# An attention layer and a routed feed-forward network on one core: constant rows of the stacks written by the engines, and three orders in the passes changed

## The reference

```
qkv = x @ W_attn + b_attn                      # 256 -> 768
scores = where(causal & (j >= i - 64), q.k / 4, -inf)
x = layernorm(x + softmax(scores) @ v @ W_proj + b_proj)
e = argmax(softmax(x @ Wr.T))                  # one expert a row
inter = gelu(x @ W1[e] + b1[e])                # 256 -> 1024
y = layernorm(inter @ Wo + bo + x) * gamma + beta
out = layernorm(x + y)
```

## Time and profile before

| | us |
|---|---|
| median of 3 runs (lowest, highest) | 550.52 (549.26, 554.35) |
| the profiled execution, its own time | 547.5 |
| its span in the profile | 545.5 |
| PE busy, share of the span | 494.5, 91% |
| DVE, ACT, POOL busy | 421.4, 353.8, 320.6 |

### The profile page before, as it was taken

How to read it: one execution, slowest core, us unless ns; L and a number is a source line. 1 busy time by engine, 2 the same in 40 slices (tenths; PEclk the granted TensorE clock), 3 DMA queues, 4 the chain that set the end, 5 groups by cost and what they waited for, 6 DMA issues and landing times. The chain is left out here.

```text
span 545.5 us, 24637 instructions
## 1 busy us (share of the span) xinstructions
PE 494.5 (91%) x8593; PEld 435.1 (80%) x8593; DVE 421.4 (77%) x1117; ACT 353.8 (65%) x800; POOL 320.6 (59%) x570
## 2 busy tenths in 40 slices
PE   4579999999999999989897899898999999999890
PEld 3458888888888888878786689897999999999780
DVE  3437888898788885886886647899999999888583
ACT  3437777768686785674756487665667667677560
POOL 7801444445453464443526456788888888888584
PEclk9959999999999997997988999999999999999896
DMA  9697676787786968687567112222343266244510
GB/s 209 166 240 190 169 205 183 225 236 183 205 217 184 248 188 219 178 227 175 145 163 194 37 42 80 61 81 71 93 100 96 81 218 228 81 146 156 179 27 14
DMA packets 97353, 83.72 MB, mean 153 GB/s; under 512 B 37447, under 2 KB 88784, under 8 KB 97235
## 3 DMA queue, kind: packets, MB, share of 16 engines
q1 hardware_dynamic: 93874, 73.70, 49.7%
q0 software_dynamic: 3264, 8.41, 4.5%
q10 hardware_dynamic: 96, 0.04, 0.0%
HBM read 43.63 MB, written 23.62 MB: 123 GB/s over the span
## 5 line engine op out<-in xcount | busy, mean ns | idle before, releaser
L1683 PE MATMUL ps<-wo_hi,ks 128*128 128x256 f16 x576 | 129.5, 274 | 4.3 <-DVE ks L1269 4.0
L1701 PE MATMUL ps<-sT_hi,w_hi 128*128 128x128 f16 x496 | 104.9, 220 | 0.4 <-issue 0.4
L1701 PE MATMUL ps<-sT_lo,w_hi 128*128 128x128 f16 x496 | 105.0, 220 | 0.0
L1701 PE MATMUL ps<-sT_hi,w_lo 128*128 128x128 f16 x496 | 105.0, 220 | 0.0
L1146 DVE TENSOR_REDUCE mx<-ps 128x4 bf16<-128x512 f32 x128 | 82.7, 683 | 8.8 <-PE ps L1469 8.2
L666 POOL CAST att_hi<-att 128x256 f16<-128x256 f32 x32 | 12.7, 396 | 123.9 <-DVE att L974 123.9
L1683 PE MATMUL ps<-wo_lo,ks 128*128 128x256 f16 x288 | 78.8, 274 | 0.0
L816 ACT ACTIVATE probs<-ps 128x512 f32<-128x512 f32 x128 | 69.4, 612 | 6.6 <-PE ps L1495 5.9
L1372 PE MATMUL ps<-v_even,probs 128*64 128x17 f32 x1024 | 71.5, 212 | 1.4 <-issue 1.4
L1372 PE MATMUL ps<-v_odd,probs 128*64 128x17 f32 x1024 | 71.5, 212 | 0.3 <-issue 0.3
L1372 PEld LDWEIGHTS ps<-v_even,probs 128*64 128x64 f32 x1024 | 66.8, 141 | 5.1 <-issue 4.5
(11 more groups left out here) (266 smaller groups left out, 1531.4 us busy)
## 6 DMA issues: line engine op xcount, KB each, us to landing
qk_s<-qk_hi SPq DMA_DIRECT2D x64, 128.0 KB, 3.0
w_in<-in_L_ffn_W_dram SPq DMA_DIRECT2D x32, 256.0 KB, 4.0
v_odd<-slots SPq DMA_DIRECT2D x62, 128.0 KB, 2.1
qs<-qk_s SPq DMA_DIRECT2D x16, 384.0 KB, 4.3
ks<-qk_s SPq DMA_DIRECT2D x16, 384.0 KB, 5.2
ks<-qk_s SPq DMA_DIRECT2D x32, 144.0 KB, 3.9
v_even<-v_odd SPq DMA_DIRECT2D x63, 68.0 KB, 4.2
qk_s<-qk_lo SPq DMA_DIRECT2D x32, 128.0 KB, 3.5
```

Source lines behind the costliest of these rows:

```text
L1683: ins = mm(ps_y[p], h[p][hs][:, ic, :], wo[ws][:, ic, :], start=n == 0, stop=n == 3 * IC - 1)
L1701: up_ins = mm(ps_h[1 - p][:, half, col + m * width:col + (m + 1) * width], weights(ws, owners[m], k, ic), sT[1 - p][ss][:, k, at], start=k ...
```

## The change

- The identity and the mask are built by POOL in the layout of the stacks, 128 rows high, `ident_w` first. DVE derives `odd` (one per row: whether it is a constant row) and copies `ident_w` over the whole of `qs[0]` and `qs[1]`. `key_rows` takes the place of `last_rows` at full height, and the `window_rows` copies now write all 128 rows of `ks`. `constant_rows` and its six DMAs are gone.
- The copies must be done before the stacks' even rows are loaded: `stacks_begin` waits for them. ACT's copies are spread over passes -4 and -3, DVE's too; POOL has one block of four copies in place of two.
- `w1` is loaded and split one pass later: half `it + 2` is loaded in pass `it`, half `it` split in it; the last split (pass 31) stands early on DVE.
- The early table is spread over passes 26, 27 and 28, in 26 and 27 behind `qk_lo`.
- In passes 28 to 31 (`ending`) the value product stands behind the transposes of the maxima, and `turn_attention` behind `scores_t(1)`.

The core of the diff:

```diff
-            sp.wait_ge(zeros_done, 1)
-            sp.wait_ge(masks_done, 1)
-            constant_rows(0)
...
                 wait(sp, st_done, 4 * (2 * g - 2))
+                if g < 2:
+                    sp.wait_ge(query_rows_done, g + 1)
+                    sp.wait_ge(window_done[g], 2)
...
-                for n in (0, 1) if it == -2 else (it + 3,) if a_tile(it + 3) and it > -2 else ():
+                n = it + 2
+                if a_tile(n):
...
-                if it == FIRST + 2:
-                    constant_rows(1)
...
+            low, high = slice(0, ALIGNED), slice(ALIGNED, P)
+            link(nc.gpsimd.memset(ident_w, 0.0))
+            link(nc.gpsimd.affine_select(out=of_copies(low, BLK), ...
+            nc.gpsimd.affine_select(out=of_copies(high, BLK), ... .then_inc(ident_w_done, 1)
...
+            for rows, per, first, last in ((low, 2, 1, P - 1), (high, 1, -STACK, P - BLK // 4)):
+                for sign, base in ((1, first), (-1, last)):
+                    link(nc.gpsimd.affine_select(out=mask_w[rows, :], ...
+            link(nc.gpsimd.affine_select(out=mask_w[high, :], ...
+            pool.wait_ge(odd_done, 1)
+            link(nc.gpsimd.tensor_scalar(mask_w[low, :], mask_w[low, :], odd[low, :], 1.0 / ONE, ALU.mult, ALU.mult))
+            for b in range(2):
+                link(nc.gpsimd.tensor_copy(key_rows[:, b, :, :, :], ...
+                nc.gpsimd.affine_select(out=key_rows[high, b, :, :, :], ... .then_inc(last_done, 1)
...
-                n = it + 1
+                n = it
                 if a_tile(n):
                     piece, cols = n // 2, slice(n % 2 * I // 2, (n % 2 + 1) * I // 2)
                     act.wait_ge(w1_ld[n % 2], 16 * (n // 2 + 1))
...
-                if it == FIRST + 1:
-                    act.wait_ge(last_done, 1)
-                    for e, t in ((0, 0), (0, 1), (1, 0), (1, 1)):
-                        last = nc.scalar.activation(window_rows(0, 0, e, t), last_rows[:, 0, :, :, :], ACT.Copy)
+                if it in (FIRST, FIRST + 1):
+                    act.wait_ge(last_done, 2)
+                    for t in range(2):
+                        last = nc.scalar.activation(window_rows(0, 1, it - FIRST, t), key_rows[:, 1, :, :, :], ACT.Copy)
...
-            nc.vector.memset(ks[0][0:ALIGNED, 0, :, 0:BLK], 0.0).then_inc(zeros_done, 1)
+            dve.wait_ge(ident_w_done, 1)
+            nc.vector.tensor_reduce(odd[:, :], ident_w[:, 0:BLK], AX.X, ALU.max).then_inc(odd_done, 1)
+            for k in range(2):
+                nc.vector.tensor_copy(qs[k][:, :, :], ident_w.unsqueeze(1).broadcast_to([P, HEADS, 2 * P]))\
+                    .then_inc(query_rows_done, 1)
...
-                if it == EARLY_OF + 2:
-                    early_runs()
-                    early_entries()
...
+                if it < EARLY_OF + 4:
+                    early_table(it)
...
+                ending = it >= TILES - LEAD
...
+                if a_tile(it + 1) and not ending:
+                    v_product(it + 1)
...
                 queries_keys(range(2 * CC))
                 if it == LAST:
                     first_up(first_owner, range(IC // 4, IC // 2))
+                elif ending:
+                    v_product(it + 1)
...
-                if it == LAST:
+                if ending:
                     turn_attention(done, ps_attT)
```

More of the change, by code:

```diff
@@ L286, in attention_then_routed_ffn @@
         xin_ld = [sem(f"xin_ld{k}") for k in range(3)]
-        rows_st = [sem(f"rows_st{k}") for k in range(2)]
+        query_rows_done = sem("query_rows_done")
         qk_st = [sem(f"qk_st{k}") for k in range(2)]
@@ L588, in _, with of_copies @@
                                     base=0, pattern=[[-1, P]], channel_multiplier=1).then_inc(ident_done, 1)
+            low, high = slice(0, ALIGNED), slice(ALIGNED, P)
+            def of_copies(rows, n):
+                return ident_w[rows, :].rearrange("p (t k) -> p t k", k=n)
+            link(nc.gpsimd.memset(ident_w, 0.0))
+            link(nc.gpsimd.affine_select(out=of_copies(low, BLK), in_=of_copies(low, BLK), compare_op=ALU.not_equal, fill=ONE,
+                                         base=-1, pattern=[[0, 4], [-2, BLK]], channel_multiplier=1))
+            nc.gpsimd.affine_select(out=of_copies(high, BLK), in_=of_copies(high, BLK), compare_op=ALU.not_equal, fill=ONE,
+                                    base=STACK, pattern=[[0, 4], [-1, BLK]], channel_multiplier=1).then_inc(ident_w_done, 1)
+            pool.wait_ge(ident_w_done, 1)
             nc.gpsimd.memset(bqk[:, :], 0.0).then_inc(bqk_clear, 1)
@@ L591, in _ @@
             link(nc.gpsimd.memset(mask_w, 0.0))
[L593 to L602, removed]
+            for rows, per, first, last in ((low, 2, 1, P - 1), (high, 1, -STACK, P - BLK // 4)):
+                for sign, base in ((1, first), (-1, last)):
+                    link(nc.gpsimd.affine_select(
+                        out=mask_w[rows, :], in_=mask_w[rows, :], compare_op=ALU.is_ge, fill=MASKED, base=base,
+                        pattern=[[sign * per, P]], channel_multiplier=-sign))
+            link(nc.gpsimd.affine_select(out=mask_w[high, :], in_=mask_w[high, :], compare_op=ALU.is_ge,
+                                         fill=0.0, base=MROWS - ALIGNED - 1, pattern=[[0, P]], channel_multiplier=-1))
+            pool.wait_ge(odd_done, 1)
+            link(nc.gpsimd.tensor_scalar(mask_w[low, :], mask_w[low, :], odd[low, :], 1.0 / ONE, ALU.mult, ALU.mult))
+            for b in range(2):
+                link(nc.gpsimd.tensor_copy(
+                    key_rows[:, b, :, :, :], mask_w.unsqueeze(1).unsqueeze(1).broadcast_to([P, STRIPS, CC, P])))
+                nc.gpsimd.affine_select(
+                    out=key_rows[high, b, :, :, :], in_=key_rows[high, b, :, :, :], compare_op=ALU.not_equal, fill=-ONE,
+                    base=ALIGNED - MROWS - STRIPS * b, pattern=[[-1, STRIPS], [-2 * STRIPS, CC], [0, P]],
+                    channel_multiplier=1).then_inc(last_done, 1)
+                pool.wait_ge(last_done, b + 1)
             link(nc.gpsimd.tensor_copy(ident_b[:, :], ident[:, :]))
@@ L1156, in router_x, with low_weights @@
                     nc.vector.tensor_tensor(lx[:, m % 4, :], ps_v[:, C:C + E], lb[:, :], ALU.add).then_inc(lx_done, 1)
+                def low_weights(n):
+                    piece, cols = n // 2, slice(n % 2 * I // 2, (n % 2 + 1) * I // 2)
+                    dve.wait_ge(w1h_done, n + 1)
+                    nc.vector.scalar_tensor_tensor(w1s[1][:, piece, cols], w1_in[:, cols], W_UP,
+                                                   w1s[0][:, piece, cols], ALU.mult, ALU.subtract)\
+                        .then_inc(w1l_done, 1)
                 maxima(0)
                 maxima(1)
+                if it == LAST:
+                    low_weights(it)
                 for t in turned(it):
@@ L1182, in _ @@
                     nc.vector.tensor_scalar(wr_in[:, :], wr_in[:, :], wr_mean[:, :], None, ALU.subtract).then_inc(centre_step, 1)
+                    dve.wait_ge(last_done, 1)
+                    for e, t in ((0, 0), (0, 1), (1, 0), (1, 1)):
+                        last = nc.vector.tensor_copy(window_rows(0, 0, e, t), key_rows[:, 0, :, :, :])
+                    last.then_inc(window_done[0], 1)
                 if it == 1:
```

109 lines of the change are left out of this document (43 added, 66 removed).

## The result

The changed kernel takes 557.15 us (median of five runs, 555.22 to 559.84); the kernel before, timed beside it, 549.26 (548.55 to 554.35). The ratio on record is 1.0246, 95% interval 1.0192 to 1.0300: slower, though whether by 2% or more stays unclear. Here that is 1.0144 with no execution left out on either side, and what makes 1.0246 of it can't be worked out from the times; that the kernel is slower doesn't hang on it, for the lowest of its five executions (555.22) lies above the highest of the kernel before (554.35). The profiled execution took 557.1 us (span 555.3) against 547.5 (545.5), 9.6 more.

What follows compares the result with a forecast made beforehand. TensorE sets the pace, so only its idle stretches and clock count. Start -4.2, early table -3.0 and end +3.4 sum to -3.8 us, taking 550.5 to 546.7; range 539.5 to 553.5.

Steps and rivals of the forecast that it cites:

- End of the passes: Passes 28 to 30: new order and late slot rows lose 3.4 us, bounds 0.5 gained and 5 lost.
- Maxima rows later by 0.7: Passes 28 to 30: `v_odd` waits for the later value product ahead of the maxima rows on ScalarE, 0.7 us late.
- 0.3 more: Passes 28 to 30: `scores_t(3)` shares a bank with `attT`, waits for turn and VectorE's copy, 0.3 us.
- For three passes 2.1: Passes 28 to 30: the new order's delays of 0.4 to 1.0 us each, 2.1 us lost together.
- Slot rows 1.3: First slot rows, queued behind the last `w1` load in pass 29, make TensorE wait 1.3 us.
- Constant rows: Start: engines replace six DMAs; stack load issued at 21.5 to 24.5 us, first scores at 27.2.
- Weights: Start: later weight units remove the 3.84 us hole; x tile 4 waits 0.5; transposes 2.3 us earlier; other passes cost nothing.
- The clock at the start: Half of 7.8 us behind the start's hole gets 2.4 GHz: 1.95 us gained, bounds none or 3.9.
- Early table: Around pass 26: spreading the table removes a wait for `qk_lo`, 3.0 us gained, bounds 0 and 3.3.
- Rival 2: Start: full-height blocks hold each other up on VectorE and GpSimd, scores near 33 us; 554.7 us, chance 0.13.
- Rival 1: Better than forecast: the end costs nothing and the clock stays high; 10.5 us faster, 540.0 us, chance 0.27.
- Rival 3: Middle passes: late stack loads in the queue give back the start's 4.2 us; 550.9 us, chance 0.18.

Runs made afterwards that it cites:

- e1: The changed kernel with TensorE's old order restored in passes 28 to 31; 547.84 us, ratio 1.0009 to the kernel before.
- after: The changed kernel itself, with all parts of the change, against the kernel before; 557.15 us, ratio 1.0246.
- e3: The changed kernel with ScalarE's `v_odd` copy behind the maxima rows in passes 28 to 31; 553.96 us, ratio 1.0081 to the kernel before.
- e7: The changed kernel with 24 unread products in each of TensorE's waits for maxima rows and slot rows; 557.04 us, ratio 1.0158 to the kernel before.
- e10: e3 plus `early_table(28)` ahead of `router_x` on VectorE and first slot rows read before the last `w1` load; 551.45 us, ratio 1.0038.
- e5: e1 plus first slot rows read ahead of the last `w1` load in pass 29; 547.68 us, ratio 0.9941 to the kernel before.
- e8: e5 plus 36, 44, 22 and 22 idle products in four TensorE waits of the start; 546.36 us, ratio 0.9946 to the kernel before.
- e9: The kernel before with only the early table spread over passes 26 to 28; 549.43 us, ratio 0.9996.
- e12: e5 plus 30, 30, 14, 14 idle products at the start and 18 before `turn_attention` in passes 28 to 30; 547.50 us, ratio 0.9938.
- e2: The kernel before with only the new order of passes 28 to 31; 557.49 us over four runs, no ratio.
- e6: The kernel before with only the weight units loaded and split one pass later; 551.76 us, ratio 1.0051.
- e4: The kernel before with only the constant rows made by the engines; 551.36 us, ratio 0.9987.

## Why the prediction was wrong

Forecast were 546.7 us and most likely no change; it is 557.15, 3.6 us above the range's upper end. Step by step:

**End of the passes: the step that failed.** The waits are the ones forecast: the value product behind the transposes, `v_odd` ahead of the maxima rows on ACT, PE waiting for them, then for DVE's copy of `attT`, then for the slot rows. e1 shows that this edit carries the loss. The term was +3.4 us, bounds -0.5 to 5; the end stretch measured +11.8. Of its parts:
- Maxima rows later by 0.7, made of 0.3 + 0.8 - 0.4: `v_odd` begins 1.11 us behind the transposes in place of 0.11, and the transposes of pass 28 follow those of pass 27 at 8.5 us in the four kernels with the new order and the spread table (after, e3, e7, e10), at 8.6 to 9.1 in the five with the old order (e1, e5, e8, e9, e12), so they do come 0.1 to 0.6 earlier. Right.
- "0.3 more" for the bank shared with `attT`: PE waits 0.38, 0.18 and 0.18 us. Right.
- For three passes 2.1: 3 x 0.84 = 2.5 by pass 28, before the earlier transposes are taken off. Right, and e2's pass 28 shows no cost at all while the clock is full.
- Slot rows 1.3: measured 1.73. (By the prediction's own numbers, rows at 304 and PE there at 301.95 + 1.4, it would have been 0.65.)
- **The clock behind these waits: nothing forecast, and it is the larger part.** This is the term that failed; the others make 3.4 us forecast and some 4 measured. I gave the start a clock term and the end none, and priced each wait at its own length. The loss by it is 5.8 to 8.5 us by e7; PE's busy time by itself grew by 10.4. None of the new waits is longer than 1.73 us; three of 1.5 stand in place of three of 1.2 or less, with the turn and the slot rows on top. Where the clock's line between enough and too little lies can't be read from these runs.

**Constant rows.** Scores at 27.2: measured 27.59. `ident_w` ready near 3.1, copies done at 5.8 to 6.6: begun at 3.23, done at 5.94. The stack load was put at 21.5 to 24.5: 22.61. `last_done` 2 was put at 11.6 to 15.0: 14.1, so POOL was late by much of the allowance. Right, as times; measured against the several profiles of the old start the part gains and loses nothing.

**Weights.** `w_hi` behind `qk_hi` of tile 3 and the hole gone, right, and shown by e6. That the later weights cost nothing in the other passes seems not to hold in pass 31 (1.46 us ahead of `first_up` in e5 in place of 0.36). The wait for x tile 4 was put at 0.5 and is 1.31. The transposes gain 1.4 us, not 2.3.

**The clock at the start.** Forecast 1.95 us gained, measured none in the two profiles: 13.7 us at 1.2 GHz either way. Over all of them it is 13.7 or 17.1 us with either start. In place of the 3.84 stand waits of 2.32, 2.74, 1.48 and 1.31 us. The bound "none" was in the range; the value was chosen as the middle between two ends, with no row for it. The other end was too low besides: it took the 7.8 us behind the hole alone, but the clock had been at 1.2 GHz since 26.1. Of 4.2 us forecast for the start, 1.9 came, and 0.9 in the two first profiles.

**Early table.** 3.0 us forecast, 2.7 measured over all profiles. The 16 us hold 327 matmuls in place of 282, at full clock, not quite the 350 named. Right.

**The rivals.** Rival 2 had the right sign and the wrong cause. Two of its three signs were there: ACT stood 1.56 us at `last_done`, and DVE's long copies took 1.3 to 1.5 us each; the third, a stack load past 25 us, was not. Its lock can be seen: POOL's memset of 128x128 took 1.16 us beside DVE's long copies, where that of 128x512 just ahead took 0.52, and DVE's four window copies took 3.27 beside POOL's copy and select but 2.16 later. The Trainium skill (SBUF — State Buffer, "Who interferes with whom") has GpSimd and a VectorE copy in a two-port mode shut each other out for an instruction's length; the trace agrees for these. But it put scores at 27.6, not 33, and e4 with all of it costs nothing that can be measured (0.9987). Rival 1 needed a clock that stays high and an end that costs nothing; both failed. (Its sum adds the 0.5 us that its end was to gain; taken off, it is -11.5 and 539.0.) Rival 3, time given back by stack loads in the middle passes, stays open: after is 4.4 us behind at pass 14 and level again at pass 26, and two profiles of the same kernel differ by 5.8 there.

**The best version** is after without the new end order and with the slot rows first (e5), 0.6% faster than the kernel before; idle products add nothing to it that can be measured.

## What to carry to other kernels

Where PE sets the pace, a new wait isn't priced by its length alone. Ask what the clock does behind it: in a stretch that already has waits, a few more of 1.5 us, with a late load, cost 3.3 to 6.0 us by their length here and 5.8 to 8.5 by the clock, as one profile each tells it. PE's busy time in the stretch gives the bound: where it works for 22.9 of 28.5 us, most of that can be added once more if the whole falls to 1.2 GHz (33.3 were measured), and that belongs in the range.

When PE's work is put in another order, the engines that read its results must be put in the same order. A change worth 2 or 3 us is lost in a scatter of 1% between executions, but shows in the length of its own stage once several profiles stand side by side.

## What the runs showed of the hardware

- With no single wait above 1.73 us, PE ran at 1.2 GHz for 32.2 of 40.3 us. In the kernel before, waits up to 1.4 us in the same passes went with 6.8 of 28.5 us, and with 0 of 27.1 in its second profile.
- With 24 idle products in each of four waits that was 3.3 of 34.5 us. They took 1.5 us at full clock and 2.32 where the clock stood at 1.2 GHz for most of them, and the median of the kernel was no lower (557.04 for 557.15).
- The second stage, from pass 31's transposes to the end, took 230.3 to 232.3 us in every profile, whatever the stretch ahead of it did; the scatter between executions lies in the passes.
